# D times the normed input: from two GpSimd passes to a diagonal matrix in TensorE's y accumulation

## The chip, the core and the metric

The kernel runs on one NeuronCore of one Trainium2 chip. The time is device microseconds of one launch, as the median of several runs. The profile is one execution, taken by the hardware profiler; its span goes from the first to the last instruction.

## What is computed

The input x has 16 sequences of 512 tokens with 128 channels, float32. The block is a state-space layer with a residual, then a mixture of experts with a residual:

```python
def _L0_attn_ref(x, A, B, C, D):
    a = jnp.diagonal(A)
    Bu = jnp.einsum('sd,bld->lbs', B, x)
    def step(h, bu_t):
        h = a * h + bu_t
        return (h, h)
    _, hs = jax.lax.scan(step, h0, Bu)
    return jnp.einsum('ds,lbs->bld', C, hs) + D * x
...
x = x + _L0_attn_ref(_layernorm(x, axis=-1), A, B, C, D)
x = x + _L0_ffn_ref(_layernorm(x, axis=-1), gate_w, shared..., r_gate, r_up, r_down)
```

So the first residual is x plus C times the states plus D times the normed x, where D is a vector of 128 numbers. The second part has a shared expert and eight routed ones, of which each token takes the one with the largest logit.

## The kernel before

There is one instruction stream for each engine, and they meet by semaphores alone; the order on each engine is the order in which its block of code issues. The work falls into three stages.

The first stage is the one that the change touches. Sixteen sequences make eight pairs q of 1024 tokens, and x of all of them stays in SBUF as x1. A pair goes through these steps, each named as its function in the code:

- norm1_stats and std1: mean and deviation of the rows (VectorE, ScalarE); norm1 writes the normed n1 (VectorE, L621).
- transpose_n1 turns n1 on TensorE (L328), copy_n1T brings it to SBUF as n1T (ScalarE, L487), bu multiplies by B (L335). The two sequences of a pair land in the lower and the upper 64 partitions of one PSUM bank.
- scan runs the recurrence over 512 steps for both sequences (VectorE, L629) and writes h, 128 partitions: 64 states of one sequence over 64 of the other.
- y multiplies by C on TensorE (L343), eight tiles of 128 tokens. Each float32 matmul leaves two records in the trace, so a y has 16.
- skip_and_input is GpSimd's: z = n1 * D (L867), then z = z + x1 (L870), each over 128 x 1024 elements.
- residual adds the y bank and z into x1 (VectorE, L637, once for each half b of the pair), and takes the stats of the result (L642, L647).
- std2, norm2_scales (r2 and nb2, L656) and norm2 (ScalarE, L494) make the second normed input n2_new. transpose_n2 (L352), split_hi (ScalarE, L502) and split_lo (VectorE, L663) make its two half-precision parts, logits multiplies by the router (L363 to L365), and route finds the expert (VectorE, L673 to L682; is_top is L678, one_hot L682).

run_pairs staggers this by hand: at its turn p each engine does the later steps of pair p and the earlier ones of p + 1 and p + 2. The first turns and the last ones are written out, those between are a loop. On VectorE a turn is

```python
has(0) and scan(p)
has(1) and norm1(p + 1)
has(0) and residual(p)
has(-1) and split_lo(p - 1)
has(0) and norm2_scales(p)
has(2) and norm1_stats(p + 2)
...
has(-1) and route(p - 1)
```

and on TensorE y(p), transpose_n1(p + 1), logits(p - 1), bu(p + 1), transpose_n2(p).

Between the second and the third pair VectorE and ScalarE prepare the weights: ScalarE writes the high halves of all experts (L511). GpSimd makes the low halves of the routed experts, with a multiply (L882) and a subtraction (L885) for each of three matrices. This stands behind its z passes in its order.

The first stage ends with one_hot of the last pair and a matmul with it (L379). The second stage does the shared expert and scatters rows into a table by expert. The third does 39 tiles of 256 table rows for the routed experts. Neither is touched by the change, but they use the memory of n1, z and n1T again.

Of the kernel before, what the change touches and what calls it, by code (L numbers as in the profile page):

```python
# [95 lines left out]
def block_kernel(nc, x, bT, cT, a_diag, d_row, gateT, weights, consts, tri_ones, token_ids, out):  # L96
# [19 lines left out]
    with ExitStack() as ctx:  # L116
# [3 lines left out]
        def sem(name):  # L120
            return ctx.enter_context(nc.semaphore(name))
# [17 lines left out]
        c_w = sb("c_w", [P, D])  # L139
        a_col = sb("a_col", [P, 1])  # L140
        d_bc = sb("d_bc", [P, D])
        eps1 = sb("eps1", [P, 1])
        eps2 = sb("eps2", [P, 1])
        w_max = sb("w_max", [P, 4])
# [78 lines left out]
        s_wlo, s_wmul, s_wlo_routed = sem("shared_weights_lo"), sem("weights_scaled"), sem("routed_weights_lo")  # L223
        s_bn1, s_mv1, s_sd1, s_r1 = sem("stats1_done"), sem("mv1_ready"), sem("sd1_ready"), sem("r1_ready")
        s_n1, s_t1, s_n1T, s_bu = sem("n1_ready"), sem("n1_transposed"), sem("n1T_ready"), sem("bu_ready")
        s_h, s_y, s_zm, s_z, s_x1 = sem("h_ready"), sem("y_ready"), sem("d_n1_ready"), sem("z_ready"), sem("x1_ready")
        s_bn2, s_mv2, s_sd2 = sem("stats2_done"), sem("mv2_ready"), sem("sd2_ready")
        s_kept = sem("n2_kept")
        s_r2, s_nb2, s_n2 = sem("r2_ready"), sem("nb2_ready"), sem("n2_ready")
# [90 lines left out]
        def _(pe):  # L320
# [16 lines left out]

            def y(q):
                pe.wait_ge(s_h, q + 1)
                for b in range(2):  # L340
                    after(pe, s_x1, q * 2 + (b - 1))
                    for t in range(BT):
                        last = mm(bank[3 + b][:, P * t:P * (t + 1)], h[N * b:N * (b + 1), P * t:P * (t + 1)],  # L343
                                  c_w[N * b:N * (b + 1), :], start=True, stop=True)
                    last.then_inc(s_y, 1)

            def transpose_n2(q):
# [123 lines left out]
        def _(act):  # L471
# [11 lines left out]
            def copy_n1T(q):  # L483
                for b in range(2):
                    act.wait_ge(s_t1, q * 2 + b + 1)
                    after(act, s_bu, q)
                    run(n1T[b][:], bank[b][:], ACT.Copy).then_inc(s_n1T, 1)  # L487

            def norm2(q):
# [92 lines left out]
        def _(dve):  # L582
# [31 lines left out]
            def norm1(q):  # L614
                dve.wait_ge(s_sd1, q + 1)
                v.reciprocal(r1[:], sd1[:]).then_inc(s_r1, 1)
                dve.wait_ge(s_r1, q + 1)
                after(dve, s_t1, q * 2)
                after(dve, s_z, q)
                for t in range(PT):  # L620
                    last = v.tensor_scalar(n1[:, t, :], x1[:, bass.ds(q * PT + t, 1), :].rearrange("p o d -> p (o d)"),  # L621
                                           mv1[:, t, 0:1], r1[:, t:t + 1], ALU.subtract, ALU.mult)
                    if t % BT == BT - 1:
                        last.then_inc(s_n1, 1)
# [5 lines left out]
                                     ALU.mult, ALU.add).then_inc(s_h, 1)  # L630

            def residual(q):
                dve.wait_ge(s_z, q + 1)
                for b in range(2):
                    dve.wait_ge(s_y, q * 2 + b + 1)
                    own = x1[:, bass.ds(q * PT + b * BT, BT), :]
                    v.tensor_tensor(out=own, in0=bank[3 + b][:].rearrange("p (t d) -> p t d", t=BT),  # L637
                                    in1=z[:, BT * b:BT * (b + 1), :], op=ALU.add).then_inc(s_x1, 1)
                dve.wait_ge(s_x1, q * 2 + 2)
                take_wait()  # L640
                for t in range(PT):
                    last = v.bn_stats(stats2[:, t, :], x1[:, bass.ds(q * PT + t, 1), :].rearrange("p o d -> p (o d)"))  # L642
                last.then_inc(s_bn2, 1)
                dve.wait_ge(s_bn2, q + 1)
                take_wait()
                for t in range(PT):
                    last = v.bn_aggr(mv2[:, t, :], stats2[:, t, :])  # L647
                last.then_inc(s_mv2, 1)
# [46 lines left out]
            def split_router():  # L695
                dve.wait_ge(s_small, 16 * SMALL)
                dve.wait_ge(s_const, 16 * 3)
                dve.wait_ge(s_wtop, 1)
                power_of_two(slice(0, 1), 0)
                dve.wait_ge(s_scale, 4)  # L700
                v.tensor_scalar(l_scale[:], w_pow[:, 0:1], 1.0 / (X_SCALE * W_SCALE), None, ALU.mult).then_inc(s_scale, 1)
                dve.wait_ge(s_whi, 1)
                v.scalar_tensor_tensor(out=router_split[:, 1, :], in0=router_f[:], scalar=w_mul[:, 0:1],
                                       in1=router_split[:, 0, :], op0=ALU.mult, op1=ALU.subtract).then_inc(s_rlo, 1)
# [151 lines left out]
        def _(pool):  # L856
# [3 lines left out]
                pool.wait_ge(s_wmax, n)  # L860
                g.partition_all_reduce(w_top[:, cols], w_max[:, cols], P, MAX_OF_PARTITIONS).then_inc(s_wtop, 1)

            def skip_and_input(q):

                pool.wait_ge(s_n1, q * 2 + 2)
                after(pool, s_x1, q * 2)
                g.tensor_tensor(out=z[:], in0=n1[:], in1=d_bc[:, None, :].to_broadcast([P, PT, D]),  # L867
                                op=ALU.mult).then_inc(s_zm, 1)
                pool.wait_ge(s_zm, q + 1)
                g.tensor_tensor(out=z[:], in0=z[:], in1=x1[:, bass.ds(q * PT, PT), :], op=ALU.add).then_inc(s_z, 1)  # L870

            weight_top(slice(0, 1), 1)
            pool.wait_ge(s_small, 16 * SMALL)
            run_pairs(pool, PAIRS, lambda p, has: has(1) and skip_and_input(p + 1),
                      between=lambda: weight_top(slice(1, 4), 2))


            pool.wait_ge(s_wlo, 3)
# [83 lines left out]
```

## Time and profile before

| | us |
|---|---|
| median of 3 runs | 449.36 |
| the runs | 447.06 to 449.62 |
| span of the profiled execution | 444.6 |
| first stage, to the matmul of L379 | 149.18 |
| VectorE busy in the span | 279.2 |
| TensorE busy in the span | 270.9 |
| GpSimd busy in the span | 206.1 |

The profiled execution is known by its span; the median lies 4.8 us above it, which takes in what lies before the first and behind the last instruction. A row of the timeline begins with the start and the duration, in us; "idle before" in brackets names the time that the engine stood, and whose end released it. Busy shares are averages over stages that are unlike each other.

### The profile page before, as it was taken

How to read it: one execution, taken by the hardware profiler on the slowest of the kernel's cores; microseconds unless marked ns; L12 is line 12 of the kernel's file. 1: busy time of each engine (PE TensorE's matmuls, PEld its weight loads, DVE VectorE, ACT ScalarE, POOL GpSimd, SP SyncE). 2: the span in 40 equal slices, each digit the busy share in tenths (PEclk: the TensorE clock that was granted, in tenths of full speed). 3: DMA queues.
4: the chain of work that ended last, by engine and by line, in shares of the span. 5: the costliest groups of instructions: out<-in, count | busy, mean ns of one | idle time of the engine just before them, and what ended most of it. 6: DMA issues, size and time to landing. Idle time of an engine off the chain costs nothing.

```text
span 444.6 us, 7851 instructions
## 1 busy us (share of the span) xinstructions
PE 270.9 (61%) x2072; PEld 193.2 (43%) x2073; DVE 279.2 (63%) x802; ACT 178.9 (40%) x368; POOL 206.1 (46%) x170
## 2 busy tenths in 40 slices
PE   0557166867752659775856723967768586867640
PEld 0334053645631235442533422745656465656530
DVE  4598898899979786663654521656365564665430
ACT  1153265453333456563645501544343343444310
POOL 0444042244499006667655751335545455545451
PEclk9999999556655669699799775988998989888955
DMA  4995505335510102223122224323424334324200
GB/s 111 393 265 189 205 2 206 130 107 174 207 47 0 49 0 81 78 77 110 71 76 97 85 85 121 81 73 103 113 78 114 89 102 114 98 80 122 61 13 0
DMA packets 48548, 46.74 MB, mean 105 GB/s; under 512 B 5359, under 2 KB 43892, under 8 KB 48144
## 3 DMA queue, kind: packets, MB, share of 16 engines
q1 hardware_dynamic: 42960, 33.64, 25.6%
q0 software_dynamic: 5568, 12.86, 8.1%
q8 instruction: 9, 0.15, 0.1%
q14 instruction: 11, 0.09, 0.1%
HBM read 18.89 MB, written 24.31 MB: 97 GB/s over the span
## 4 chain that ended last, share of the span: by engine, by line
PE 35%; DVE 24%; issue 15%; another core or an unknown queue 8%; ACT 6%; POOL 4%; DMA 3%; DVEq 2%; ACTq 0%; SPq 0%; POOLq 0%
PE bank L431 6%; PE bank L343 4%; PE bank L430 4%; PE bank L429 4%; PE bank L417 3%; PE bank L446 2%; PE bank L447 2%; DVE stats L642 2%; PE bank L448 2%; DVE n2T_lo L663 2%; DVE stats L606 2%; DVE is_top L678 2%; DVE w_full L844 2%; POOL table L892 2%
## 5 line engine op out<-in xcount | busy, mean ns | idle before, releaser
L903 POOL DMA_INDIRECT out<-w_full,result_id x78 | 80.1, 1027 | 87.1 <-DVE w_full L844 69.4
L446 PE MATMUL bank<-w_split,hid_hi 128*128 x156 | 34.2, 239 | 36.2 <-DVE w_full L844 35.3
L892 POOL DMA_INDIRECT table<-rows,row_place x32 | 33.1, 1033 | 38.3 <-DVE rows L803 30.1
L867 POOL TENSOR_TENSOR z<-n,d_bc 128x1024 f32<-128x1024 f32 x8 | 18.8, 2344 | 64.4 <-DVE x L637 57.0
L430 PE MATMUL bank<-xT_lo,w_split 128*128 128x256 f16 x156 | 46.9, 301 | 0.5 <-issue 0.5
L429 PE MATMUL bank<-xT_hi,w_split 128*128 128x256 f16 x156 | 46.9, 301 | 0.4 <-issue 0.4
L431 PE MATMUL bank<-xT_hi,w_split 128*128 128x256 f16 x156 | 46.8, 300 | 0.5 <-issue 0.5
L563 ACT ACTIVATE xT_hi<-bank 128x256 f16<-128x256 f32 x39 | 14.9, 383 | 76.2 <-PE bank L417 50.0
L403 PE MATMUL bank<-w_split,hid_hi 128*128 128x128 f16 x128 | 27.3, 245 | 28.6 <-DVE hid_lo L794 28.6
L831 DVE SCALAR_TENSOR_TENSOR z<-bank,h_scale,n 128x512 f32<-128x512 f32 x26 | 19.5, 751 | 38.3 <-PE bank L431 20.3
L892 POOL DMA_INDIRECT table<-w_full,row_place x32 | 31.6, 988 | 20.2 <-DVE w_full L803 10.8
L343 PE MATMUL bank<-c_w,h 64*128 64x128 f32 x128 | 23.3, 418 | 22.2 <-DVE h L629 22.2
L446 PEld LDWEIGHTS bank<-w_split,hid_hi 128*128 128x128 f16 x156 | 16.6, 106 | 42.3 <-issue 41.6
L534 ACT ACTIVATE n<-bank,g_scale 128x512 f32<-128x512 f32 x32 | 21.0, 683 | 33.3 <-remote 23.2
L494 ACT ACTIVATE n_new<-x,nb,r 128x128 f32<-128x128 f32 (+1 forms) x64 | 25.5, 480 | 20.8 <-DVE nb L656 20.8
L447 PE MATMUL bank<-w_split,hid_hi 128*128 x156 | 33.2, 238 | 0.0
L448 PE MATMUL bank<-w_split,hid_lo 128*128 x156 | 32.9, 237 | 0.0
L343 PEld LDWEIGHTS bank<-c_w,h 64*128 64x128 f32 x128 | 21.1, 307 | 26.4 <-issue 15.2
L389 PE MATMUL bank<-n2T_hi,w_split 128*128 128x512 f16 (+1 forms) x64 | 27.0, 422 | 6.0 <-DVE z L787 6.0
L403 PEld LDWEIGHTS bank<-w_split,hid_hi 128*128 128x128 f16 x128 | 14.3, 111 | 33.3 <-DVE hid_lo L794 28.9
L417 PE MATMUL bank<-identity,w_full 128*128 128x128 f32 x78 | 18.0, 316 | 16.9 <-DMA w_full<-table 12.4
L787 DVE SCALAR_TENSOR_TENSOR z<-bank,h_scale,n 128x512 f32<-128x512 f32 x32 | 23.1, 747 | 7.3 <-ACT n L534 3.2
(123 smaller groups left out, 794.6 us busy)
## 6 DMA issues: line engine op xcount, KB each, us to landing
table<-pad_row SPq DMA_DIRECT2D x6, 1716.0 KB, 7.7
w_full<-table SPq DMA_DIRECT2D x39, 136.0 KB
w_full<-table SPq DMA_DIRECT2D x39, 128.0 KB
x<-in_x SPq DMA_DIRECT2D x8, 512.0 KB, 7.3
n<-n_new SPq DMA_DIRECT2D x8, 512.0 KB, 3.1
w_full<-in_weights SPq DMA_DIRECT2D x3, 1152.0 KB, 9.6
out<-w_full,result_id POOLq DMA_INDIRECT x78
table<-rows,row_place POOLq DMA_INDIRECT x32
```

Of the source, the lines that this page charges most:

```text
L343: last = mm(bank[3 + b][:, P * t:P * (t + 1)], h[N * b:N * (b + 1), P * t:P * (t + 1)], c_w[N * b:N * (b + 1), :], start=True, stop=True)
L389: mm(o, w_split[:, kind, 0, 0, f], n2T_hi[:, tok], start=True, stop=False)
L403: mm(o, hi, w_split[:, 2, 0, 0, f], start=(c == 0), stop=False)
L417: last = nc.tensor.transpose(bank[0][:, P * s:P * (s + 1)], x_in[k][:, s, :], identity[:])
L429: mm(o, w_hi, xT_hi[k][:], start=True, stop=False)
L430: mm(o, w_hi, xT_lo[k][:], start=False, stop=False)
L431: last = mm(o, w_of(kind, e, 1, c), xT_hi[k][:], start=False, stop=True)
L446: mm(o, hid_hi[k][:, slot], w_of(2, e, 0, c), start=(c == 0), stop=False)
L447: mm(o, hid_hi[k][:, slot], w_of(2, e, 1, c), start=False, stop=False)
L448: last = mm(o, hid_lo[k][:, slot], w_of(2, e, 0, c), start=False, stop=(c == FC - 1))
L892: g.indirect_dma_start(table[:, :], bass.IndirectOffsetOnAxis(ap=row_place[k][:, t:t + 1], axis=0), rows[k][:, t, :], None).then_inc(s_sca ...
L903: g.indirect_dma_start(out_rows[:, :], bass.IndirectOffsetOnAxis(ap=result_id[k][:, s:s + 1], axis=0), result[k][:, s, :], None, bounds_ch ...
```

## The change

GpSimd's skip_and_input is gone, and with it z in this stage. VectorE builds a matrix d_diag once, which has D on its diagonal. In y each tile first takes a matmul of the turned normed input n1T with d_diag, which gives n1 * D with tokens back on the partitions, and the product with C is added to it in the same bank. The residual adds the bank to x1 in place. norm1 no longer waits for z, and copy_n1T waits for the y of the pair before, which now reads n1T.

```diff
@@ -139,6 +139,7 @@
         c_w = sb("c_w", [P, D])
         a_col = sb("a_col", [P, 1])
         d_bc = sb("d_bc", [P, D])
+        d_diag = sb("d_diag", [P, D])
         eps1 = sb("eps1", [P, 1])
         eps2 = sb("eps2", [P, 1])
         w_max = sb("w_max", [P, 4])
@@ -223,7 +224,7 @@
         s_wlo, s_wmul, s_wlo_routed = sem("shared_weights_lo"), sem("weights_scaled"), sem("routed_weights_lo")
         s_bn1, s_mv1, s_sd1, s_r1 = sem("stats1_done"), sem("mv1_ready"), sem("sd1_ready"), sem("r1_ready")
         s_n1, s_t1, s_n1T, s_bu = sem("n1_ready"), sem("n1_transposed"), sem("n1T_ready"), sem("bu_ready")
-        s_h, s_y, s_zm, s_z, s_x1 = sem("h_ready"), sem("y_ready"), sem("d_n1_ready"), sem("z_ready"), sem("x1_ready")
+        s_h, s_y, s_diag, s_x1 = sem("h_ready"), sem("y_ready"), sem("d_diag_ready"), sem("x1_ready")
         s_bn2, s_mv2, s_sd2 = sem("stats2_done"), sem("mv2_ready"), sem("sd2_ready")
         s_kept = sem("n2_kept")
         s_r2, s_nb2, s_n2 = sem("r2_ready"), sem("nb2_ready"), sem("n2_ready")
@@ -337,11 +338,14 @@
 
             def y(q):
                 pe.wait_ge(s_h, q + 1)
+                if isinstance(q, int) and q == 0:
+                    pe.wait_ge(s_diag, 1)
                 for b in range(2):
                     after(pe, s_x1, q * 2 + (b - 1))
                     for t in range(BT):
-                        last = mm(bank[3 + b][:, P * t:P * (t + 1)], h[N * b:N * (b + 1), P * t:P * (t + 1)],
-                                  c_w[N * b:N * (b + 1), :], start=True, stop=True)
+                        o, tok = bank[3 + b][:, P * t:P * (t + 1)], slice(P * t, P * (t + 1))
+                        mm(o, n1T[b][:, tok], d_diag[:], start=True, stop=False)
+                        last = mm(o, h[N * b:N * (b + 1), tok], c_w[N * b:N * (b + 1), :], start=False, stop=True)
                     last.then_inc(s_y, 1)
 
             def transpose_n2(q):
@@ -484,6 +488,7 @@
                 for b in range(2):
                     act.wait_ge(s_t1, q * 2 + b + 1)
                     after(act, s_bu, q)
+                    after(act, s_y, q * 2)
                     run(n1T[b][:], bank[b][:], ACT.Copy).then_inc(s_n1T, 1)
 
             def norm2(q):
@@ -616,7 +621,6 @@
                 v.reciprocal(r1[:], sd1[:]).then_inc(s_r1, 1)
                 dve.wait_ge(s_r1, q + 1)
                 after(dve, s_t1, q * 2)
-                after(dve, s_z, q)
                 for t in range(PT):
                     last = v.tensor_scalar(n1[:, t, :], x1[:, bass.ds(q * PT + t, 1), :].rearrange("p o d -> p (o d)"),
                                            mv1[:, t, 0:1], r1[:, t:t + 1], ALU.subtract, ALU.mult)
@@ -630,12 +634,11 @@
                                      ALU.mult, ALU.add).then_inc(s_h, 1)
 
             def residual(q):
-                dve.wait_ge(s_z, q + 1)
                 for b in range(2):
                     dve.wait_ge(s_y, q * 2 + b + 1)
                     own = x1[:, bass.ds(q * PT + b * BT, BT), :]
                     v.tensor_tensor(out=own, in0=bank[3 + b][:].rearrange("p (t d) -> p t d", t=BT),
-                                    in1=z[:, BT * b:BT * (b + 1), :], op=ALU.add).then_inc(s_x1, 1)
+                                    in1=own, op=ALU.add).then_inc(s_x1, 1)
                 dve.wait_ge(s_x1, q * 2 + 2)
                 take_wait()
                 for t in range(PT):
@@ -695,6 +698,7 @@
             def split_router():
                 dve.wait_ge(s_small, 16 * SMALL)
                 dve.wait_ge(s_const, 16 * 3)
+                v.tensor_tensor(out=d_diag[:], in0=identity[:], in1=d_bc[:], op=ALU.mult).then_inc(s_diag, 1)
                 dve.wait_ge(s_wtop, 1)
                 power_of_two(slice(0, 1), 0)
                 dve.wait_ge(s_scale, 4)
@@ -860,19 +864,9 @@
                 pool.wait_ge(s_wmax, n)
                 g.partition_all_reduce(w_top[:, cols], w_max[:, cols], P, MAX_OF_PARTITIONS).then_inc(s_wtop, 1)
 
-            def skip_and_input(q):
-
-                pool.wait_ge(s_n1, q * 2 + 2)
-                after(pool, s_x1, q * 2)
-                g.tensor_tensor(out=z[:], in0=n1[:], in1=d_bc[:, None, :].to_broadcast([P, PT, D]),
-                                op=ALU.mult).then_inc(s_zm, 1)
-                pool.wait_ge(s_zm, q + 1)
-                g.tensor_tensor(out=z[:], in0=z[:], in1=x1[:, bass.ds(q * PT, PT), :], op=ALU.add).then_inc(s_z, 1)
-
             weight_top(slice(0, 1), 1)
             pool.wait_ge(s_small, 16 * SMALL)
-            run_pairs(pool, PAIRS, lambda p, has: has(1) and skip_and_input(p + 1),
-                      between=lambda: weight_top(slice(1, 4), 2))
+            weight_top(slice(1, 4), 2)
 
 
             pool.wait_ge(s_wlo, 3)
```

On TensorE, from the first pair's bu to the second pair's y. bank is a PSUM bank, b_w and c_w are B and C turned, n_new is the second normed input. Before:

```order
L335 MATMUL bank<-n1T,b_w 64x512 x2
L343 MATMUL bank<-c_w,h 128x128 x8
L328 MATMUL bank<-identity,n 128x128 x8
L335 MATMUL bank<-n1T,b_w 64x512 x2
L352 MATMUL bank<-identity,n_new 128x128 x8
```

And now, from inside the first pair's y:

```order
12 L347 MATMUL bank<-d_diag,n1T 128x128
13 L348 MATMUL bank<-c_w,h 128x128
14 L347 MATMUL bank<-d_diag,n1T 128x128
15 L348 MATMUL bank<-c_w,h 128x128
16 L347 MATMUL bank<-d_diag,n1T 128x128
17 L348 MATMUL bank<-c_w,h 128x128
18 L347 MATMUL bank<-d_diag,n1T 128x128
19 L348 MATMUL bank<-c_w,h 128x128
20 L329 MATMUL bank<-identity,n 128x128 x8
21 L336 MATMUL bank<-n1T,b_w 64x512 x2
22 L356 MATMUL bank<-identity,n_new 128x128 x8
```

Eight matmuls with d_diag stand between the eight with c_w; nothing else on this engine moved.

On GpSimd, from the loop over the pairs to the last of the weights' passes (w_full is the weights as loaded, w_split their halves). Before:

```order
23 L870 TENSOR_TENSOR z<-z,x 128x1024
24 L56 REGISTER_ALU
25 L56 COMPARE_AND_BRANCH
26 L867 TENSOR_TENSOR z<-n,d_bc 128x1024
27 L870 TENSOR_TENSOR z<-z,x 128x1024
28 L882 TENSOR_TENSOR w_full<-w_full,w_mul 128x2048
29 L885 TENSOR_TENSOR w_split<-w_full,w_split 128x8x256
30 L882 TENSOR_TENSOR w_full<-w_full,w_mul 128x2048
31 L885 TENSOR_TENSOR w_split<-w_full,w_split 128x8x256
32 L882 TENSOR_TENSOR w_full<-w_full,w_mul 128x2048
33 L885 TENSOR_TENSOR w_split<-w_full,w_split 128x8x256
```

And now, from the search for the largest weight:

```order
7 L865 ISA w_top<-w_max 128x1
8 L865 ISA w_top<-w_max 128x3
9 L876 ISA
10 L876 TENSOR_TENSOR w_full<-w_full,w_mul 128x2048
11 L879 TENSOR_TENSOR w_split<-w_full,w_split 128x8x256
12 L876 TENSOR_TENSOR w_full<-w_full,w_mul 128x2048
13 L879 TENSOR_TENSOR w_split<-w_full,w_split 128x8x256
14 L876 TENSOR_TENSOR w_full<-w_full,w_mul 128x2048
15 L879 TENSOR_TENSOR w_split<-w_full,w_split 128x8x256
```

The weights' passes now follow directly on that search, with no pair in between.

## Rows read from the trace of the kernel before

**Rows 1.** The page: busy share of an engine; granted TensorE clock in 40 slices.
```profile
PE 270.9 (61%) x2072; PEld 193.2 (43%) x2073; DVE 279.2 (63%) x802; ACT 178.9 (40%) x368; POOL 206.1 (46%) x170
...
PEclk9999999556655669699799775988998989888955
```

**Rows 2.** Timeline of one loop pair: start us, us, engine, line, operation, idle before.
```profile
85.38 3.09 PE L343 MATMUL bank<-c_w,h 64*128 64x128 f32 x16 [0.61 <-DVE h L629]
85.66 2.14 DVE L621 TENSOR_SCALAR n<-x,mv,r 128x128 f32 x8 [0.33 <-DVE r L616]
...
88.39 1.97 PE L328 MATMUL bank<-identity,n 128*128 128x128 f32 x8
88.62 0.69 DVE L637 TENSOR_TENSOR x<-bank,z 128x512 f32 x1 [0.22 <-PE bank L343]
...
91.59 1.26 DVE L663 TENSOR_TENSOR n2T_lo<-bank,n2T_hi 128x512 f32 x2
...
92.00 2.34 POOL L870 TENSOR_TENSOR z<-z,x 128x1024 f32<-128x1024 f32 x1 [0.19 <-POOL z L867]
...
92.99 1.37 DVE L656 SCALAR_TENSOR_TENSOR nb<-mv,r 128x8 f32<-128x8 f32 x1
...
93.09 0.18 PE L363 MATMUL bank<-router_split,n2T_hi 128*128 128x8 f16 x1 [2.72 <-DVE n2T_lo L663]
...
95.06 1.98 PE L335 MATMUL bank<-n1T,b_w 128*64 128x512 f32 x4
...
96.97 1.97 PE L352 MATMUL bank<-identity,n_new 128*128 128x128 f32 x8
97.00 0.22 DVE L678 TENSOR_TENSOR is_top<-is_top,expert_less_E 128x64 f32<-128x64 f32 x1
...
99.57 3.09 PE L343 MATMUL bank<-c_w,h 64*128 64x128 f32 x16 [0.64 <-DVE h L629]
```

**Rows 3.** Timeline of the pairs before the loop and of its first.
```profile
26.44 1.97 DVE L656 SCALAR_TENSOR_TENSOR nb<-mv,r 128x8 f32<-128x8 f32 x1
...
55.15 5.77 ACT L511 ACTIVATE w_split<-w_full,w_mul 128x2048 f16<-128x2048 f32 x3
...
57.21 3.09 PE L343 MATMUL bank<-c_w,h 64*128 64x128 f32 x16 [11.25 <-DVE h L629]
...
71.48 1.70 PE L343 MATMUL bank<-c_w,h 64*128 64x128 f32 x16 [0.99 <-DVE h L629]
```

**Rows 4.** Timeline of the last two pairs and of the first stage's end.
```profile
113.36 3.09 PE L343 MATMUL bank<-c_w,h 64*128 64x128 f32 x16 [0.19 <-DVE h L629]
...
122.05 3.60 POOL L882 TENSOR_TENSOR w_full<-w_full,w_mul 128x2048 f32<-128x2048 f32 x1
...
122.54 3.19 DVE L678 TENSOR_TENSOR is_top<-is_top,expert_less_E 128x64 f32<-128x64 f32 x1
...
125.73 4.05 POOL L885 TENSOR_TENSOR w_split<-w_full,w_split 128x2048 f16<-128x2048 f32 x1
...
126.02 3.84 DVE L682 TENSOR_TENSOR one_hot<-expert_less_E,first_top 128x64 f16<-128x64 f32 x1
...
131.04 3.09 PE L343 MATMUL bank<-c_w,h 64*128 64x128 f32 x16 [4.46 <-DVE h L629]
133.22 0.69 DVE L637 TENSOR_TENSOR x<-bank,z 128x512 f32<-128x512 f32 x1 [2.23 <-PE bank L343]
...
134.18 0.69 DVE L637 TENSOR_TENSOR x<-bank,z 128x512 f32<-128x512 f32 x1 [0.26 <-PE bank L343]
...
138.55 2.51 DVE L656 SCALAR_TENSOR_TENSOR nb<-mv,r 128x8 f32<-128x8 f32 x1
...
149.18 0.61 PE L379 MATMUL bank<-one_hot,tri 128*128 128x512 f16 x1 [1.35 <-DVE one_hot L682]
```

**Rows 5.** Stretches: length, busy of PE, PEld, DVE, ACT, POOL; PEclk, DMA, GB/s.
```profile
85.30:88.50 3.20, 3.12 (x17) 2.90 (x18) 2.78 (x10) 0.20 (x1) 0.00 (x0) 0.50 1.00 343
...
102.70:107.00 4.30, 1.72 (x8) 1.46 (x8) 4.10 (x22) 1.50 (x3) 3.16 (x2) 0.83 0.69 230
```

## The prediction

> **What bounds the kernel now.** I read the page's busy shares first: VectorE is busy 279.2 of 444.6 us, but that is an average over stages [rows 1]. The edit touches only the first stage, up to the ranks' matmul at 149.18 [rows 4]; what follows can only start later or earlier by whatever this stage ends later or earlier. So the second view is the timeline of one loop pair, from the y at 85.38 to the y at 99.57 [rows 2]. See two chains that run round it. One is VectorE alone: residual, stats, scales, routing, scan. The other crosses: y (3.09 us) on TensorE, then the second residual add, which ends at 88.62 + 0.69 = 89.31, the stats, the low half of n2T (91.59 + 1.26 = 92.85), logits (93.09), bu (95.06), the transposes of n2 (96.97 + 1.97 = 98.94), and the next y. The leg of 14.19 us is 3.93 from y's start to 89.31, and 10.26 from there to the next y.
>
> In those 10.26 us see the row of nb2: eight numbers per partition take 1.37 us, from 92.99 to 94.36, and GpSimd's add of x into z runs from 92.00 to 94.34. An operation eight times as wide, is_top at 97.00, takes 0.22. So nb2 stands still until GpSimd is done: 1.17 us lost per pair. The same shows at larger size where GpSimd splits the routed weights [rows 4]: is_top 3.19, one_hot 3.84, nb2 2.51, all on VectorE's own order ahead of the scan or of n2.
>
> **The change part by part.**
>
> *Sixteen more matmul records in each y.* All eight y of 16 records become 32. At the low clock (0.50 granted, 1.2 GHz) 16 records take 3.09 [rows 2, 5]. Doubling gives 6.2 us, the low bound. But y's halves overlap now: the first half is handed over 2.18 us after the start and the second only 0.96 later (131.04, 133.22, 134.18, [rows 4]), since they use the upper and the lower 64 rows of the array. The diagonal matmuls use all 128 rows and stand between, so I expect no overlap. Eight records in 2.18, with some 0.45 of that the way out to VectorE, is 0.21 each: 32 x 0.21 + 0.3 = 7.0 us, my price at the low clock. The other bound is the 128-row transposes, 1.97 for 8 records, 0.246 each: 7.9. At the high clock (2.4 GHz, nine tenths or more in the slice from 67 to 78 us [rows 1]) the y at 71.48 took 1.70 [rows 3]; doubled and rounded up, 3.6.
>
> *Which clock.* The nines that the profile's page shows before 67 us [rows 1] are not borne out by the work: the y at 57.21 took the 3.09 that it also takes at 0.50 [rows 3, 5]. Of the y rows only that at 71.48 was fast; it came behind bu and transposes. The clock also rose behind y and the transposes after it (0.83 in 102.70 to 107.00), when TensorE then had nothing to do [rows 5]. So before the change the clock rises just too late for y. With twice the work in y it should rise inside it. I take 6.5 us for the first four y, which come after idle time, 4.5 for the next three, which follow bu and transposes without a gap, and 5.0 for the last. That is a choice between 3.6 and 7.0. The Trainium skill (TensorE: Matmul & The Clock Gate, Part 1) says that the default state is throttled and activity releases the throttle; by that alone every y should come out at 3.6, which is the second rival below.
>
> *Who waits.* VectorE's norm1 (2.14 us from 85.66) covers no more of y than it covers now; the second residual add must come after all 32 records. From y's start to its end costs Y + 0.8 instead of 3.9. Four times (6.5 + 0.8 - 3.9) = 13.6 (13.9, since the y at 71.48 was fast and its stretch 3.6), three times 1.4 = 4.2, once 1.9: 20.0 us longer. The diagonal itself (one 128x128 multiply ahead of the first scan) adds 0.2, by is_top's 0.22 for half the width and the 0.69 of a 512-wide add. The wait of ScalarE's copies on the previous y costs nothing: TensorE does that y before the transposes they read. The wait of norm1 on z goes too, but y ends after norm1 anyway.
>
> *GpSimd's 16 passes go.* nb2 no longer stands. In the first pair 1.97 - 0.2 = 1.8 comes back [rows 3], in the second about 1.1. In the three plain loop legs VectorE's chain shrinks from 10.26 to 9.1, but the crossing chain ends at 98.94 - 89.31 = 9.6, of which the next matmul overlaps 0.1 (88.39 against 85.38 + 3.09). So 9.5 is late next and a leg gives back 0.76, three of them 2.3.
>
> *The weights' passes move.* They stood behind the z passes in GpSimd's order, at 122 to 145 us. Now they wait only for ScalarE's high halves, done at 55.15 + 5.77 = 60.9 [rows 3], call it S: 3.7 us after the y at 57.21. They are three times 3.60 and 4.05 [rows 4], so about 23 us, with borders at S + 3.7, 7.7, 11.4, 15.4, 19.1 and 23.1. In that pair, with Y = 6.5, nb2 comes at S - 3.7 + 6.5 + 0.8 + 3.7 = S + 7.3 and stands to 7.7. is_top comes 2.6 later (97.00 - 94.36) and stands from 10.3 to 11.4; one_hot, 0.5 behind it, to 15.4. That is 4.9 of stalls on 9.1: 14.0 instead of 71.48 - 57.21 - 3.9 = 10.4, a loss of 3.6. In return the tail is free: the leg from 113.36 to 131.04 is 13.8 behind its 3.9 us. Without stalls its n2 transposes end and the next y starts some 8.3 after the residual (nb2's end 3.8, the eight n2 rows 3.3, four transposes 1.1): 5.5 back. In the last leg nb2's 2.51 becomes 0.2: 2.3 back. The is_top of the last leg had time to spare.
>
> *The sum.* 20.0 + 0.2 + 3.6 - 1.8 - 1.1 - 2.3 - 5.5 - 2.3 = +10.8 us. The profiled span of 444.6 becomes 455.4. The median of the runs, 449.36, lies 4.8 above that span; I let this offset stand: **460 us**.
>
> **The rivals.**
>
> *The clock stays low through y.* Against a rise speaks that 3.09 us of y alone raised nothing at 57.21 or 85.38. Then Y = 7.0 everywhere. Four times 0.5 more, three times 2.5 and once 2.0: 11.5. nb2 of the third pair then slips past the border at S + 7.7 and the stalls shift to the next ones, 3.7 more. In all +26: 475 us.
>
> *The clock is high in every y.* For it speaks the y at 71.48. With 3.6 the eight y cost 8 x 0.5 = 4.0 instead of 20.0; of the crossing chain bu and transposes halve, so the loop legs fall to VectorE's 9.1 (1.2 more back in three), and n2's transposes give 0.4. But nb2 of the third pair comes at S + 4.4 and stands longer, 2.9 more, to the same border. +10.8 - 16.0 - 1.6 + 2.9 = -3.9: 445.5 us, not slower. The place is y's second half: the point from which the change stops costing is where the mean Y falls to about 5.5 - 10.8/8 = 4.2 us.
>
> *The weights' passes hide.* If VectorE meets them only in operations that don't block, the 4.9 of stalls go: 455 us. Against it: is_top, one_hot and nb2 blocked each time that GpSimd was in a big pass, and the third pair has all three.
>
> *norm1 is blocked as well.* No row shows norm1 beside a GpSimd pass. In the fourth pair, from S + 17.5, it meets the fifth and sixth; at worst it ends at S + 25.2 instead of 20, and 1.5 us outlast y: 462. The Trainium skill (GPSIMD Engine Reference, the spec table's SBUF interfaces) names both kinds, instructions with two SBUF inputs, which the rows show, and those in a two-port mode, which norm1 may be and the rows don't show; by its rule this rival holds.
>
> **How the numbers follow.** Forecast (clock rises inside y) 0.55, its own range 453 to 467. Clock low throughout 0.15; clock high throughout 0.12; weights hidden 0.10; norm1 blocked 0.08. 1% is 4.5 us, about what these runs can tell from no change: slower is above 453.9, faster below 444.9. Slower: 0.53 of the forecast's 0.55, all of the low clock, half of the hidden, all of the blocked: 0.81. Faster: a third of the high clock, 0.04. Same: 0.15. The range leaves out the worst of the low clock and most of the high clock: 449 to 472.
>
> **What would show it.** In the new profile y should be 32 records, and the second residual add should wait on it for some 2 us in each pair. nb2 should be 0.2 us in pairs without a weights pass. GpSimd's six passes should start near 64 us, and is_top and one_hot of the third pair should be the long ones. The stage's last matmul, 149.18 before, should start near 160. The forecast is wrong if y rows come out near 3.6 throughout, if y's halves still overlap (6.2 at the low clock), or if the stage after 149 doesn't just shift.

## The result and the profile after

The changed kernel takes 494.6 us, the one before 448.6 beside it: ratio 1.1047, 95% interval 1.0992 to 1.1103. It is 46.0 us slower. 460 us had been forecast. Its profiled execution took 492.8 us, 2.3 more than its span of 490.5; so most of the 4.8 us that stand between median and span before is the spread between executions, not what lies before the first and behind the last instruction.

The page of the changed kernel, its busy shares and three of its groups (busy us, mean ns | idle before, releaser):

```profile
PE 327.1 (67%) x2200; PEld 226.3 (46%) x2201; DVE 266.1 (54%) x803; ACT 178.9 (36%) x368; POOL 169.2 (34%) x154
...
L347 PE MATMUL bank<-d_diag,n1T 128*128 128x128 f32 x128 | 43.6, 437 | 19.0 <-DVE h L633 19.0
...
L348 PE MATMUL bank<-c_w,h 64*128 64x128 f32 x128 | 43.5, 433 | 0.0
L640 DVE TENSOR_TENSOR x<-bank,x 128x512 f32<-128x512 f32 (+1 forms) x16 | 11.1, 692 | 59.0 <-PE bank L348 59.0
```

y is now two groups of 128 records, 437 and 433 ns each. The third group has the new big number: VectorE's residual waits 59.0 us for y, where it waited 4.3 us in all before. VectorE's share falls from 63% [rows 1] to 54%.

The timeline of the third pair, whose y answers to the one at 57.21 [rows 3], and of the routing behind it:

```profile
69.45 0.79 PE L347 MATMUL bank<-d_diag,n1T 128*128 128x128 f32 x2 [11.28 <-DVE h L633]
...
70.17 0.79 PE L348 MATMUL bank<-c_w,h 64*128 64x128 f32 x2
...
70.89 0.79 PE L347 MATMUL bank<-d_diag,n1T 128*128 128x128 f32 x2
...
75.46 0.69 DVE L640 TENSOR_TENSOR x<-bank,x 128x512 f32 x1 [3.29 <-PE bank L348]
...
81.02 1.97 PE L329 MATMUL bank<-identity,n 128*128 128x128 f32 x8
81.25 0.69 DVE L640 TENSOR_TENSOR x<-bank,x 128x512 f32 x1 [5.10 <-PE bank L348]
...
84.22 1.25 DVE L666 TENSOR_TENSOR n2T_lo<-bank,n2T_hi 128x512 f32 x2
...
84.69 4.06 POOL L879 TENSOR_TENSOR w_split<-w_full,w_split 128x2048 f16<-128x2048 f32 x1
...
85.62 3.15 DVE L659 SCALAR_TENSOR_TENSOR nb<-mv,r 128x8 f32<-128x8 f32 x1
...
91.40 0.98 DVE L681 TENSOR_TENSOR is_top<-is_top,expert_less_E 128x64 f32<-128x64 f32 x1
...
92.80 3.73 DVE L685 TENSOR_TENSOR one_hot<-expert_less_E,first_top 128x64 f32 x1 [0.16 <-DVE first_top L683]
...
98.13 2.14 DVE L625 TENSOR_SCALAR n<-x,mv,r 128x128 f32 x8 [0.39 <-DVE r L621]
```

See the starts of y's rows: 0.72 us from one matmul (two records) to the next, so 0.36 a record, and 11.57 us from 69.45 to the transposes at 81.02. Before it was 88.39 - 85.38 = 3.01 [rows 2]. VectorE's second add waits 5.10 for it, where some 2 had been expected. Further down stand GpSimd's pass at 84.69 and with it nb2 (3.15), then is_top (0.98) and one_hot (3.73); norm1 at 98.13 comes after the last pass and keeps its 2.14.

TensorE loads the stationary operand of each matmul by an instruction of its own (PEld). These loads in the same y:

```profile
70.17 0.50 PEld L348 LDWEIGHTS bank<-c_w,h 64*128 64x128 f32 x2 [0.23 <-issue]
70.89 0.50 PEld L347 LDWEIGHTS bank<-d_diag,n1T 128*128 128x128 f32 x2 [0.22 <-issue]
```

Each pair of loads starts with its matmul and not ahead of it, and before each the loading stood for 0.22 us. e8 below shows the same loads without this.

TensorE in the fifth pair, which follows bu and transposes without a gap:

```profile
121.17 0.48 PE L348 MATMUL bank<-c_w,h 64*128 64x128 f32 x2
121.58 0.49 PE L347 MATMUL bank<-d_diag,n1T 128*128 128x128 f32 x2
122.00 0.49 PE L348 MATMUL bank<-c_w,h 64*128 64x128 f32 x2
...
126.58 1.09 PE L329 MATMUL bank<-identity,n 128*128 128x128 f32 x8
```

Here a matmul comes every 0.417 us and the transposes too are fast (1.09, against 1.97 [rows 2]). VectorE beside and behind it:

```profile
113.96 0.17 DVE L659 SCALAR_TENSOR_TENSOR nb<-mv,r 128x8 f32<-128x8 f32 x1
...
126.81 0.69 DVE L640 TENSOR_TENSOR x<-bank,x 128x512 f32 x1 [2.64 <-PE bank L348]
```

nb2 stands no longer: 0.17, against 1.37 [rows 2]. The clock over three of the y (length, busy of PE, PEld, DVE, ACT, POOL, then PEclk, DMA share, GB/s):

```profile
97.80:109.40 11.60, 11.60 (x33) 8.01 (x33) 2.83 (x9) 0.00 (x0) 0.00 (x0) 1.00 0.19 64
117.00:127.00 10.00, 10.00 (x48) 7.06 (x45) 4.82 (x15) 1.89 (x5) 0.00 (x0) 1.00 0.66 230
...
169.00:181.30 12.30, 12.24 (x37) 8.58 (x36) 0.93 (x3) 1.19 (x2) 0.00 (x0) 0.50 0.11 44
```

As before, the 1.00 that is shown for the early part is not borne out by the work: the y from 97.80 took 11.6 us like the one from 169.00 with 0.50 granted. The eight y last 11.6, 11.5, 11.6, 11.6, 7.0, 6.9, 6.9 and 11.5 us. The first stage ends at

```profile
193.85 0.61 PE L383 MATMUL bank<-one_hot,tri 128*128 128x512 f16 x1 [1.35 <-DVE one_hot L685]
```

which answers to 149.18 [rows 4]: 44.7 us later, and what lies behind it (490.5 - 193.85 = 296.6 us, before 295.4) is longer by 1.2 us. So nearly the whole loss is in the first stage.

### The profile page after: what moved, and what is told of

Same layout as the page of the kernel before. It is cut to its first block, busy times and chain, and to the rows that moved or that the text cites. A ratio compares the mean times of both kernels' runs of the same rounds, so it can differ in the third digit from the quotient of the medians.

```text
span 490.5 us, 8047 instructions
## 1 busy us (share of the span) xinstructions
PE 327.1 (67%) x2200; PEld 226.3 (46%) x2201; DVE 266.1 (54%) x803; ACT 178.9 (36%) x368; POOL 169.2 (34%) x154
## 4 chain that ended last, share of the span: by engine, by line
PE 41%; issue 33%; DVE 14%; DMA 4%; SPq 2%; ACT 2%; POOL 1%; DVEq 1%; another core or an unknown queue 1%; POOLq 0%; ACTq 0%
PE bank L348 8%; PE bank L347 8%; PE bank L435 6%; PE bank L434 4%; PE bank L433 4%; PE bank L421 3%; DMA w_full<-table 3%; DVE stats L645 2%; PE bank L356 2%; PE bank L450 2%; DVE n2T_lo L666 2%; PE bank L451 2%; PE bank L336 2%; DVE w_max L713 2%; DVE w_full L848 1%
## 5 line engine op out<-in xcount | busy, mean ns | idle before, releaser
L450 PE MATMUL bank<-w_split,hid_hi 128*128 x156 | 33.5, 236 | 38.0 <-DVE w_full L848 38.0
L347 PE MATMUL bank<-d_diag,n1T 128*128 128x128 f32 x128 | 43.6, 437 | 19.0 <-DVE h L633 19.0
L348 PE MATMUL bank<-c_w,h 64*128 64x128 f32 x128 | 43.5, 433 | 0.0
L640 DVE TENSOR_TENSOR x<-bank,x 128x512 f32<-128x512 f32 (+1 forms) x16 | 11.1, 692 | 59.0 <-PE bank L348 59.0
L347 PEld LDWEIGHTS bank<-d_diag,n1T 128*128 128x128 f32 x128 | 28.0, 272 | 31.8 <-issue 24.4
L835 DVE SCALAR_TENSOR_TENSOR z<-bank,h_scale,n 128x512 f32<-128x512 f32 x26 | 19.5, 751 | 38.2 <-PE bank L435 27.4
L886 POOL DMA_INDIRECT table<-w_full,row_place x32 | 32.9, 1029 | 18.2 <-DVE w_full L807 9.7
L450 PEld LDWEIGHTS bank<-w_split,hid_hi 128*128 128x128 f16 x156 | 16.4, 105 | 44.7 <-issue 43.7
L492 ACT ACTIVATE n1T<-bank 128x512 f32<-128x512 f32 x16 | 9.2, 596 | 75.2 <-PE bank L329 75.2
L348 PEld LDWEIGHTS bank<-c_w,h 64*128 64x128 f32 x128 | 27.1, 264 | 12.2 <-issue 9.7
L451 PE MATMUL bank<-w_split,hid_hi 128*128 x156 | 32.6, 235 | 0.0
```

The costliest lines, as they stand in the source:

```text
L347: mm(o, n1T[b][:, tok], d_diag[:], start=True, stop=False)
L348: last = mm(o, h[N * b:N * (b + 1), tok], c_w[N * b:N * (b + 1), :], start=False, stop=True)
L450: mm(o, hid_hi[k][:, slot], w_of(2, e, 0, c), start=(c == 0), stop=False)
L451: mm(o, hid_hi[k][:, slot], w_of(2, e, 1, c), start=False, stop=False)
L886: g.indirect_dma_start(table[:, :], bass.IndirectOffsetOnAxis(ap=row_place[k][:, t:t + 1], axis=0), rows[k][:, t, :], None).then_inc(s_sca ...
```

## The experiments

The first eight ran on two chips on which the kernel before takes 378.9 and 378.7 us instead of 448.6; the last three on one where it takes 448.8. The difference lies behind the first stage (see e13 at the end), so a ratio from one chip doesn't stand for another. The table gives the difference in microseconds too, and the end of the first stage in the one profile of each kernel (the start of the matmul that is at 149.18 before). The stage alone varies from profile to profile of one kernel: by 4.9 us for the changed one, by 1.1 for the one before.

| kernel | ratio to before, interval | us against before | first stage ends |
|---|---|---|---|
| before | 1 | 0 | 149.2, again 148.1 |
| changed | 1.1047 (1.0992 to 1.1103) | +46.0 | 193.9 |
| changed again (e7) | 1.1172 (1.1085 to 1.1259) | +46.2 | 198.8 |
| e1 no diagonal | 0.9869 (0.9818 to 0.9921) | -4.2 | 145.8 |
| e2 diagonal only | one run, 374.36 against 378.94 us | -4.6 | 146.5 |
| e3 grouped | 1.0378 (1.0326 to 1.0430) | +14.8 | 166.6 |
| e6 weights held | 1.1007 (1.0970 to 1.1044) | +38.0 | 192.4 |
| e8 full rows | 1.0176 (1.0099 to 1.0254) | +8.2 | 156.5 |
| e9 diagonal first | 1.0051 (1.0019 to 1.0083) | +2.6 | 151.6 |
| e10 diagonal in gap | 0.9827 (0.9751 to 0.9903) | -5.1 | 143.6 |
| e11 in gap, weights held | 0.9788 (0.9745 to 0.9831) | -10.1 | 140.5 |
| e12 in gap, weights spread | 0.9599 (0.9554 to 0.9644) | -18.7 | 129.1 |

At a margin of 2%, the changed kernel, e3, e6 and e12 differ clearly from the one before. The others lie within the margin or their interval reaches across it.

**e1: the added matmuls alone taken out.**

```diff
-                        mm(o, n1T[b][:, tok], d_diag[:], start=True, stop=False)
-                        last = mm(o, h[N * b:N * (b + 1), tok], c_w[N * b:N * (b + 1), :], start=False, stop=True)
+                        last = mm(o, h[N * b:N * (b + 1), tok], c_w[N * b:N * (b + 1), :], start=True, stop=True)
```

> The changed kernel without the eight diagonal matmuls in each y; D times the normed input is left out of the sum. GpSimd's passes stay gone. If the added matmuls are the whole loss, y is back at 3.1 us at the low clock, the span of the first stage falls from 193.9 to near 140 us and the time to about 440 us, below the kernel before (448.6) by what GpSimd's passes had blocked, 9 us by the prediction's terms. Rival: something else of the change (the in-place residual, the wait of the copies, the moved weights' passes) costs, and the time stays above 448 us.

y is back at 3.09 us and the kernel is faster than before, by 1.3%: the added matmuls are more than the whole loss. But the first stage ends only 3.4 us earlier than before, not 9. The timeline at the fourth pair shows one place where the rest went, GpSimd's passes with norm1 among them:

```profile
72.42 3.60 POOL L875 TENSOR_TENSOR w_full<-w_full,w_mul 128x2048 f32<-128x2048 f32 x1
...
74.16 7.62 DVE L624 TENSOR_SCALAR n<-x,mv,r 128x128 f32 x8 [0.39 <-DVE r L620]
76.10 4.05 POOL L878 TENSOR_TENSOR w_split<-w_full,w_split 128x2048 f16<-128x2048 f32 x1
```

norm1 takes 7.62 us instead of 2.14 [rows 2] beside GpSimd's last two passes and ends 1.6 us after them. In the changed kernel the passes were over by then.

**e2: the diagonal matmuls without those with C.**

```diff
-                        mm(o, n1T[b][:, tok], d_diag[:], start=True, stop=False)
-                        last = mm(o, h[N * b:N * (b + 1), tok], c_w[N * b:N * (b + 1), :], start=False, stop=True)
+                        last = mm(o, n1T[b][:, tok], d_diag[:], start=True, stop=True)
```

> The changed kernel with only the diagonal matmuls in y; the product of the states with C is left out. The scan is still waited for. Theory A: a float32 matmul over all 128 rows can't have its weight load hidden, whatever its neighbour: the 16 records stay at 0.36 us each at the low clock, y is 5.8 us. Theory B: only the alternation between a 128-row and a 64-row matmul costs; alone the diagonal ones run at 0.21 to 0.25 each, y is 3.4 to 4.0 us.

The same y, of the third pair, at the low clock:

```profile
53.17 3.78 PE L347 MATMUL bank<-d_diag,n1T 128*128 128x128 f32 x16 [11.28 <-DVE h L632]
```

Sixteen records in 3.78 us, or 3.57 to the start of the next instruction. Theory A falls: a 128-row float32 matmul among its like costs 0.22 to 0.24 a record, next to what the prediction had. Alone the diagonal part is 3.8 and alone the part with C is 3.1; alternating they are 11.6.

**e3: four of the one kind, then four of the other.**

```diff
-                        mm(o, n1T[b][:, tok], d_diag[:], start=True, stop=False)
-                        last = mm(o, h[N * b:N * (b + 1), tok], c_w[N * b:N * (b + 1), :], start=False, stop=True)
+                        mm(o, n1T[b][:, tok], d_diag[:], start=(t == 0), stop=False)
+                    for t in range(BT):
...
+                        last = mm(o, h[N * b:N * (b + 1), tok], c_w[N * b:N * (b + 1), :], start=False, stop=(t == BT - 1))
```

> The changed kernel with four diagonal matmuls in a row and then four with C, in each half. Theory A: the four diagonal ones still take 0.72 each (2.9 us), the four with C fall back to 0.4 each: y about 9.2 us at the low clock, some 12 us less in all. Theory B: y about 7 us, some 25 us less in all. If neither is so and every matmul keeps 0.72 us (y 11.6), the loads are held up by something that grouping doesn't touch.

TensorE in the third pair's y:

```profile
62.68 2.07 PE L347 MATMUL bank<-d_diag,n1T 128*128 128x128 f32 x8 [11.28 <-DVE h L635]
64.68 2.07 PE L350 MATMUL bank<-c_w,h 64*128 64x128 f32 x8
66.68 2.07 PE L347 MATMUL bank<-d_diag,n1T 128*128 128x128 f32 x8
68.69 2.07 PE L350 MATMUL bank<-c_w,h 64*128 64x128 f32 x8
```

Both kinds take 2.00 us from group to group. y is 8.1, between the two theories' numbers. Neither was right as written: B had left the changes that remain at no cost, while 8 records of 0.2135 are 1.71, and the 0.29 that is left comes once for each group. In the changed kernel a matmul of two records costs 0.723: 0.427 and 0.296, once for each matmul. The same number at both places is what one change between a 128-row and a 64-row matmul costs. A change from the lower 64 rows to the upper 64, as the kernel before has it once in each y, adds nothing: its eight matmuls take 3.01 us, less than 8 x 0.427 = 3.42.

**e8: no change of rows at all, same records, same order.**

```diff
-                        last = mm(o, h[N * b:N * (b + 1), tok], c_w[N * b:N * (b + 1), :], start=False, stop=True)
+                        last = mm(o, h[:, tok], c_full[:, b, :], start=False, stop=True)
```

c_full holds C in the upper rows for one half and in the lower for the other, and zeros elsewhere; VectorE fills it once.

> The changed kernel with C padded by zeros to 128 rows, so that the matmul with C too uses the whole array; the records and their order stay as in the changed kernel. Theory: each change between a 128-row and a 64-row matmul costs some 0.30 us at the low clock and 0.21 at the high one, on top of 0.21 (0.107) a record: y falls from 11.6 to 7.1 us (6.9 to 3.7), the first stage ends near 160 us instead of 194, and the time is some 10 us above the kernel before, as the prediction had it. Rival: the cost lies in alternating two stationary operands or in the accumulation itself: y stays near 11.6.

TensorE in the third pair's y, at its middle and at its end, then two of its weight loads, then the clock over its first 4.4 us and its end:

```profile
61.30 0.63 PE L349 MATMUL bank<-c_full,h 128*128 128x128 f32 x2
61.72 0.64 PE L348 MATMUL bank<-d_diag,n1T 128*128 128x128 f32 x2
...
64.07 0.39 PE L348 MATMUL bank<-d_diag,n1T 128*128 128x128 f32 x2
64.30 0.39 PE L349 MATMUL bank<-c_full,h 128*128 128x128 f32 x2
```

```profile
61.09 0.55 PEld L349 LDWEIGHTS bank<-c_full,h 128*128 128x128 f32 x2
61.52 0.55 PEld L348 LDWEIGHTS bank<-d_diag,n1T 128*128 128x128 f32 x2
```

```profile
59.00:63.40 4.40, 4.39 (x20) 4.40 (x21) 2.60 (x9) 3.35 (x2) 0.90 (x1) 0.50 0.00 0
63.80:65.00 1.20, 1.20 (x13) 1.20 (x12) 0.00 (x0) 0.00 (x0) 1.20 (x1) 0.99 0.00 0
```

The rows come 0.427 us apart at the low clock and 0.223 at the high one. Neither a stationary operand of its own for each matmul, nor alternating the moving one between d_diag and C, nor adding in the bank costs anything; the change of rows does, 0.296 at the low clock and 0.417 - 0.223 = 0.194 at the high one. The loads show how: here each starts 0.21 us ahead of its matmul (61.09 and 61.30, 61.52 and 61.72) and the loading never stands, in the changed kernel none starts ahead across a change. That is 0.21 of the 0.296. And now the clock rises inside y, from 0.50 granted to 0.99, between these two pairs of rows. The eight y take 5.6, 5.5, 6.1, 6.2, 3.8, 3.8, 3.8 and 5.7 us. The stage ends 7.4 us later than before, the kernel is 1.8% slower. Beside GpSimd's last two passes norm1 of the fourth pair took 7.76 us here, and that pair's residual came some 2.3 us later for it.

**e6: where the weights' passes stand.**

```diff
+            pool.wait_ge(s_x1, 2 * PAIRS - 2)
             pool.wait_ge(s_wlo, 3)
```

> The changed kernel with GpSimd's six weights' passes held back until the seventh pair's residual, about where they stood before. By the prediction the third pair loses its stalls (7.2 us in the changed profile: 3.0 at nb2, 0.8 at is_top, 3.5 at one_hot) and the last two pairs take on about as much (8.9 before): within 3 us of the changed kernel. Rival: the stalls of the third pair are hidden by the long y, and holding the passes back makes it slower by 5 us or more.

The stage ends 1.4 us earlier than in the first profile of the changed kernel. The stalls only change place: is_top 2.98 and one_hot 3.27 between the y of the last two pairs, none in the third. In time the expectation missed: e6 is 38.0 us above the kernel before, the changed one 46.0 and 46.2. The profile doesn't settle where the rest went, since its execution was the longest of the five (422.9 us, the others 416.1 to 417.4). **e7** was the changed kernel itself beside the others.

> The changed kernel once more, beside the kernel before on the chip of this call, as the base for the others here. Expected: the first stage ends near 194 us again and the kernel is slower than the one before by about 45 us; the two kernels may both be faster than in the first measurement, since the chip of the first experiments ran the kernel before in 378.9 us.

It came out 46 us slower again (424.9 against 378.7). Its stage ends 4.9 us later than in the first profile, by one y: the fifth was at the low clock this time, 11.5 instead of 7.0.

**e9: the diagonal ones first, ahead of the wait on the scan.**

```diff
             def y(q):
-                pe.wait_ge(s_h, q + 1)
...
                         o, tok = bank[3 + b][:, P * t:P * (t + 1)], slice(P * t, P * (t + 1))
-                        mm(o, n1T[b][:, tok], d_diag[:], start=True, stop=False)
-                        last = mm(o, h[N * b:N * (b + 1), tok], c_w[N * b:N * (b + 1), :], start=False, stop=True)
+                        mm(o, n1T[b][:, tok], d_diag[:], start=(t == 0), stop=False)
+                pe.wait_ge(s_h, q + 1)
+                for b in range(2):
+                    for t in range(BT):
+                        o, tok = bank[3 + b][:, P * t:P * (t + 1)], slice(P * t, P * (t + 1))
+                        last = mm(o, h[N * b:N * (b + 1), tok], c_w[N * b:N * (b + 1), :], start=False, stop=(t == BT - 1))
```

> The changed kernel with all eight diagonal matmuls ahead of the wait on the scan, and the eight with C behind it. Where TensorE stands before y (the first four pairs) the diagonal part is hidden and 3.1 us are left behind the wait; in the loop 3.5 us (1.7 at the high clock) come on the chain. Two changes of row mode in a pair instead of sixteen. First stage near 152 us, time within 1% of the kernel before. Rival: in the loop they delay every y by their full length and the stage ends above 160 us.

As expected, 0.5% slower than before. **e10** puts the same eight between the transposes of the pair and the logits; for the first pair they stand behind bu.

```diff
                 has(1) and transpose_n1(p + 1),
+                has(1) and not early(p) and skip(p + 1),
                 has(-1) and logits(p - 1),
                 has(1) and bu(p + 1),
+                has(1) and early(p) and skip(p + 1),
```

> As e9, but the diagonal matmuls of the next pair stand between its transposes and the logits, where TensorE had nothing to do for 2.7 us. They need the copies of n1T, so some 1 to 2 us of them delay logits and bu at the low clock, nothing at the high one. First stage near 148 us, time at or just below the kernel before; no better than the kernel without the diagonal (145.8).

TensorE in the loop (logits stand between 98 and 101):

```profile
91.39 3.09 PE L354 MATMUL bank<-c_w,h 64*128 64x128 f32 x16 [0.44 <-DVE h L644]
94.42 1.90 PE L329 MATMUL bank<-identity,n 128*128 128x128 f32 x8
96.22 2.05 PE L347 MATMUL bank<-d_diag,n1T 128*128 128x128 f32 x16
...
101.09 1.08 PE L336 MATMUL bank<-n1T,b_w 128*64 128x512 f32 x4
...
104.36 1.71 PE L354 MATMUL bank<-c_w,h 64*128 64x128 f32 x16 [1.09 <-DVE h L644]
```

The diagonal ones (96.22) are fast and fit into the gap. bu behind them takes 1.08 and the next y 1.71, at the high clock. It is 1.7% faster than before. Its stage ends 2 us ahead of that of e1, which hasn't the diagonal at all, but that is one profile each, and the intervals of their times overlap: that e10 is the faster one isn't shown, nor that the filled gap kept the clock up, since in e13 four y were fast with the gap unfilled.

**e11 and e12: what GpSimd's passes still cost.** e11 is e10 with the wait of e6. e12 releases each pass by itself:

```diff
+                pool.wait_ge(s_n1, 2 * (4 + 2 * i))
                 g.tensor_tensor(out=full, in0=full, in1=w_mul[:, 1 + k:2 + k].to_broadcast([P, E * F]),
...
                 pool.wait_ge(s_wmul, i + 1)
+                pool.wait_ge(*((s_n1, 2 * (5 + 2 * i)) if i < 2 else (s_y, 2 * PAIRS)))
                 g.tensor_tensor(out=w_split[:, k, 1:, 1, :], in0=full.rearrange("p (e f) -> p e f", e=E),
```

> e10 with GpSimd's six weights' passes held back until the seventh pair's residual, as in e6. In e10 the stretch from the third pair's y to the fifth's is 39.0 us where plain pairs take 26, 13 us of stalls in nb2, one_hot, is_top and norm1. Held back, these go and about 9 us come at the end (before: 3.0, 3.6 and 2.3): first stage near 140 us, time 1% below e10. Rival: since the end has nothing to hide behind, all 13 come back there, and it is no faster than e10.

> e10 with each of the six passes (3.60 or 4.05 us) released by itself: the first five when norm1 of the fourth to the eighth pair is done, the last at the last pair's second half of y. Between norm1 and nb2 VectorE has some 5 us in which no operation reads two operands from SBUF or runs norm1. If these are the only ones that stand beside GpSimd, nearly all of e10's 13 us go: first stage near 132 us, time near 362 us where e10 has 373.6. Rival: the stats and the reads from PSUM are slowed as well, or the last pass ends the stage: above 140 us.

GpSimd in e12, three of the six passes:

```profile
67.67 4.08 POOL L892 TENSOR_TENSOR w_split<-w_full,w_split 128x2048 f16<-128x2048 f32 x1 [8.27 <-DVE n L636]
80.51 3.60 POOL L888 TENSOR_TENSOR w_full<-w_full,w_mul 128x2048 f32<-128x2048 f32 x1 [8.76 <-DVE n L636]
...
116.56 4.06 POOL L892 TENSOR_TENSOR w_split<-w_full,w_split 128x2048 f16<-128x2048 f32 x1 [7.56 <-PE bank L354]
```

VectorE in the same kernel beside the pass at 80.51:

```profile
78.29 2.14 DVE L636 TENSOR_SCALAR n<-x,mv,r 128x128 f32 x8 [0.38 <-DVE r L632]
...
81.87 1.44 DVE L656 BATCH_NORM_STATS2 stats<-x 128x6 f32 x7
...
83.90 1.25 DVE L677 TENSOR_TENSOR n2T_lo<-bank,n2T_hi 128x512 f32 x2
...
85.30 0.17 DVE L670 SCALAR_TENSOR_TENSOR nb<-mv,r 128x8 f32<-128x8 f32 x1
```

norm1 (78.29) is done before the pass, the stats run beside it in the 1.44 us that they also take in the changed kernel at 127.75, where GpSimd does nothing, and nb2 comes at 85.30, after its end at 84.11. The low half of n2T meets this pass for 0.2 us only; that it isn't held up is shown by the changed kernel, where it takes 1.25 us at 84.22 beside a pass and the same 1.25 at 112.56 without one. nb2, is_top, one_hot and norm1 all have their short durations in e12. e11's stage is 3.2 us shorter than e10's, which is no more than two profiles of one kernel differ by, e12's 14.6. e12 is the fastest of all: 4.0% below the kernel before, and 8.6 us below e11 on the same chip.

> The kernel before, once more with a profile, on the chip of these experiments. Expected: the first stage ends near 149 us as in the first profile, and the 70 us between 448.6 and 378.7 lie behind it, in the stages that the change doesn't touch.

e13's stage ended at 148.1. It took 448.0 us, on a chip where the kernel before takes 448.8, so it can't show where the 70 us lie. The changed kernel does: behind its stage are 296.6 us in the first profile and 426.2 - 198.8 = 227.4 in e7's. Four of its y, from the fourth to the seventh pair, took 1.7 us where the first profile had that once, and the stage was still only 1 us shorter.

## Why the prediction was wrong

**The step that failed is the price of the added records.** "32 x 0.21 + 0.3 = 7.0 us, my price at the low clock", with 7.9 as the other bound. It came out at 11.6, above both, and 6.9 instead of 3.6 at the high clock. The 0.21 was right (0.2135 in e8), and so was the loss of the overlap of y's halves. What was missing is a term, put at nothing without a reason: sixteen changes between the 128-row diagonal and the 64-row matmul with C, 0.296 us each at the low clock and 0.194 at the high, so 4.7 or 3.1 us in each y. At each change the next weight load waits instead of running beside the matmul ahead of it. The Trainium skill (TensorEngine Tiling (Array Packing), Key Properties) says that changing the tiling mode drains TensorE. It gives no price; e3 and e8 give one. The trace agrees in so far as no load runs ahead across a change. I had seen that the two halves overlap and that the diagonal would part them. I took what stands between them as a loss of overlap, and didn't ask what it costs to go from the one mode to the other.

**The second part is the clock.** For the first four y I took 6.5 us, because with more work the clock would rise inside them. In e8, with the changes of rows gone, it did rise inside them: they take 5.5 to 6.2, the middle ones 3.8 where I had 4.5, the last 5.7 where I had 5.0. In the changed kernel the clock rose in none of the first four, though TensorE's matmul records left no gap for 11.6 us (97.80 to 109.40 above); the loads filled 8.0 of it, where they filled all of y in e8. In e3, with four changes in a y instead of sixteen, it stayed at 0.50 for the 8.0 us of the third and the fourth y as well. That the changes keep the clock down is likely by this; what about them does it isn't shown. Which of the three middle ones are at the high clock varies with the run (e7).

**The sum.** From y's start to the end of the second residual the eight pairs took 84.9 us, before 31.6: +53.3 where the prediction had +20.0. The rest of the stage is 44.7 - 53.3 = -8.6, where its terms gave 0.2 + 3.6 - 13.0 = -9.2. The five y at the low clock have 80 changes, the three at the high one 48: 80 x 0.296 + 48 x 0.194 = 33.0 us. Without them +20.3 is left, next to the +20.0. That is in part luck: at the clock that it ran at, y would be 6.9 instead of 6.5 and 5.0 in the first four and the last, and 3.8 instead of 4.5 in the three between, and these cancel. So nearly the whole error is this one term. Inside the rest two terms were off against each other. The first y started 0.85 us earlier than before (17.95 against 18.80), where 0.2 later was forecast, and the third pair cost 5.5 us and not 3.6. Its stalls were 3.0, 0.8 and 3.5 = 7.2, not 4.9, since the longer y brought nb2 to other borders of GpSimd's passes. The free tail gave what was forecast: the leg behind the seventh pair's residual is 169.76 - 161.65 = 8.1 (8.3 in the prediction), nb2 0.17.

**The rivals.** The low clock in all y held for five of eight, the high clock in all for three. The weights' passes didn't hide. norm1 is blocked by them, as the fourth rival had it: not in the changed kernel, but in e1 (7.62 us) and e8 (7.76 us). By the Trainium skill's rule (GPSIMD Engine Reference, the spec table's SBUF interfaces) that would follow if norm1 runs in a two-port mode; the stall agrees with it, but no row names the mode. That e1 gained 3.4 us and not 9 lies in two pairs: from y to y its third takes 20.7 us and its fourth 18.7, 6.4 and 4.8 more than before. nb2, is_top and one_hot of the third took 8.7 us, 0.6 of it their own, and norm1 of the fourth 5.5 more than its 2.14. Everywhere else e1 gained 14.6 us.

With the prediction's own price made true, in e8, the stage ends 7.4 us later than before and the time is 8.2 us longer: near the +10.8 that were forecast.

## What to carry to other kernels

Before adding matmuls to an accumulation, compare how many rows of the array each uses: between neighbours that differ, a change has a price of its own, here 0.30 us beside the 0.43 of the matmul itself, and more than the work that was added. Group them by row count or pad the small one, and put what doesn't need the late operand where the engine waits anyway. Long GpSimd passes over SBUF belong beside VectorE operations that read from PSUM or take stats: releasing them one by one (e12) shortened the stage by 11.4 us against holding them all back (e11).

## What the runs showed of the hardware

- A change between a 64-row and a 128-row float32 matmul costs 0.30 us at the low clock and 0.19 at the high one; matmuls over the same rows, each with a stationary operand of its own, follow at 0.427 and 0.223 us. Over the same rows a weight load starts 0.21 us ahead of its matmul (e8); across a change it starts with it, and the loading stands for 0.22 us before (changed kernel, e3).
- With such a change after each matmul TensorE's matmul records show no gap, and yet the clock stayed at 1.2 GHz for 11.4 us (0.50 granted in e7's fourth y and in the changed kernel's last); with the same number of records and no changes the granted clock was 0.50 from 59.00 to 63.40 and 0.99 from 63.80 (e8).
- VectorE's norm1, one tensor from SBUF to SBUF with two scalars per partition, stands still beside a GpSimd pass (7.62 us instead of 2.14). bn_stats (1.44 us beside a pass and without one) and a subtraction with one operand in PSUM (1.25 us both times) don't.
- The same kernel before took 448.6 to 448.8 us on some chips and 378.7 to 378.9 on others, and the kernel before was profiled only on the former. The changed kernel's two profiles put the difference behind the first stage: 297 us there on a chip of the one kind, 227 on one of the other, with first stages of 194 and 199. What makes that difference stayed open.
